# Scores of the next step beside the weights, value sums behind the masked scores, and the first batch of x in four pieces

## The chip, the cores and the metric

The kernel runs on one core of a Trainium2 chip. The metric is the device time of one execution in microseconds; less is better. Engines are named as in the profile: PE multiplies matrices (PEld is its weight load), DVE, ACT and POOL do elementwise work, SP issues DMA transfers.

## The reference

One decoder layer on x of 4 batches, 512 tokens, 512 features, in fp32. The part that the change touches is the first sublayer, a gated attention with 16 heads and 64 memory slots:

```python
def step_k(hk, x):
    q_t, k_t, p_t, g_t = x
    hk = hk * g_t[:, :, None, :] + k_t[..., None] * p_t[:, :, None, :]
    return (hk, jnp.einsum('bhk,bhkm->bhm', q_t, hk))
...
pvT = jax.nn.softmax(okT, axis=-1)
def step_v(hv, x):
    pv_t, v_t, p_t, g_t = x
    hv = hv * g_t[..., None] + p_t[..., None] * v_t[:, :, None, :]
    return (hv, jnp.einsum('bhm,bhmv->bhv', pv_t, hv))
...
o = o * jax.lax.rsqrt(jnp.mean(jnp.square(o), axis=-1, keepdims=True) + EPS) * g_norm_weight
o = o * (g * jax.nn.sigmoid(g))
return o.reshape(b, t, VALUE_DIM) @ Wo
```

q, k, s, v and g are projections of x. A cross attention over a context of 512 tokens and an MLP with quantised weights and activations and two Hadamard transforms follow, each with a residual and a layer norm.

## The kernel before

The program is written by hand, engine by engine, with semaphores; each engine walks the same list of stages (`attention_order`, then `seam_order`, then `ffn_order`) and emits its own part of each.

**Steps.** The first sublayer is 32 steps. A step is a pair of heads of one batch. The recurrences are done as sums over four blocks of 128 tokens, with a triangular mask inside a block. Step n's own stages are: `keys` (transposes of k and of exp(s)), `scores` (k times q for each head, 128x128 per block, masked by DVE into AM), `states` (running sums of k times p in HK, L485, and of p times v in HV, L490), `ok` (HK times q, L497, and exp(s) times the masked scores, L502, into one bank), `turn_ok`, a softmax, `turn_w`, `weights` (exp(s) times the softmax weights, L526, masked by DVE into the same AM, and HV times the weights, L534), `values` (AM times V, L540). Between them stand projections of step n+1 (`q`, `k`, `s`, `vg0` to `vg3`: 12 matmuls of 128x512 each, L431 to L433, three passes of a split fp32 product) and the output of step n-1 (`turn_o`, `y`: 24 such matmuls). The tuple `STEP` is this order; `OF_NEXT` names the stages that belong to step n+1.

**Shapes on PE.** Three kinds of matmul use the array differently. Most use all of it. `scores` and `weights` contract over 64 rows, one head in each half of the rows, side by side in time (64*128 in the profile: the row tiling). L490 and L502 write 64 columns for each head (128*64: the column tiling). In the profile two instructions stand for each matmul of an fp32 product with 128 columns.

**Banks.** PE's `take` hands out eight PSUM banks by due times from a table, `HOLD`; a bank is reused once the reader of its last content has counted its semaphore.

**Masks.** DVE's part of `scores` multiplies both heads' scores by the mask (L1008), its part of `weights` does it for the weights (L1048). In `values` it sums squares, POOL takes the root (L1337), then DVE gates the output (L1061).

**Beside the steps.** From step 24 on, `PLACES` puts the stages of the cross attention of each batch at numbered places (16 a step) of the stage list. `SEAM` is the order of the last step. `UNIT` is the order in the MLP. `tern` stages prepare the MLP's weights in the RAW buffers.

**Start.** SP first loads constants (C) and three vectors, then the list `first`: Wq, batch 0 of x in two halves (into AM and OG, free at that time), Wk, Ws, Wv and Wg, batch 1 of x, Wo. ACT rounds each piece to its high part, DVE subtracts to make the low part. A projection starts when all of x's batch and its weights have both parts.

Of the kernel before, what the change touches and what calls it, by code (L numbers as in the profile page):

```python
# [10 lines left out]
ALU = mybir.AluOpType  # L11
# [3 lines left out]
NB, T, D = 4, 512, 512  # L15
# [21 lines left out]
class Queue:  # L37
# [5 lines left out]
    def wait_ge(self, sem, value):  # L43
# [5 lines left out]
STEP = ("keys", "q", "scores", "states", "load_x", "tern", "k", "ok", "s", "turn_ok", "turn_o", "vg0", "tern",  # L49
        "turn_w", "vg1", "y", "weights", "vg2", "values", "tern", "vg3")  # L50
OF_NEXT = ("q", "k", "s", "vg0", "vg1", "vg2", "vg3")


def step_order(n, tasks):

    terns = 0
    for stage in STEP:
        m = n + 1 if stage in OF_NEXT else n - 1 if stage in ("turn_o", "y") else n
        if stage == "tern":
            terns += 1  # L60
            if n and terns in ((2,) if n + 1 in LAST else (1, 2, 3)):
                for t in tasks[:1]:
                    yield stage, t
                del tasks[:1]
        elif stage == "load_x":
            if n == 0:
                yield stage, 3
        elif 0 <= m < STEPS:
            yield stage, m
# [26 lines left out]

PLACED = [stage for stage in STEP if stage not in ("scores", "load_x", "tern")]


def attention_order():  # L100
# [3 lines left out]
    yield "load_x", 2  # L104
# [8 lines left out]
SEAM = (("keys", 31), ("scores", 31), ("states", 31), ("turn_o", 30), ("ok", 31), ("y", 30), ("turn_ok", 31), None,  # L113
# [7 lines left out]
def seam_order():  # L121

    for p, item in enumerate(SEAM):
        if item and item[0] == "unit":
            yield from ffn_place(item[1])
        elif item:
# [6 lines left out]
    dict(ctx=400, centre=403, n1=406, qk=408, qk_out=409, x101=414, x101_out=415, energy=418, x123=419,  # L133
         energy_out=419, att_scale=419, x123_out=420, att01=422, att01_out=423, att23=424, att23_out=426, xm0=430,
         xm0_out=431, xm1=433, xm1_out=434, xm2=435, xm2_out=436, xm3=438, xm3_out=439, x_round0=440, x_made0=443,
         x_round1=443, x_made1=445, x_turned=449, x_turned_out=450),
    dict(ctx=445, centre=445, qk=447, qk_out=448, n1=449, x101=450, energy=451, x101_out=452, energy_out=452,
         x123=454, att_scale=454, x123_out=455, att01=456, att01_out=457, att23=457, att23_out=458, xm0=459,
         xm0_out=461, xm1=463, xm1_out=464, xm2=464, xm2_out=465, xm3=465, xm3_out=466, x_round0=467, x_made0=468,
         x_round1=468, x_made1=471, x_turned=475, x_turned_out=476),  # L140
    dict(ctx=475, centre=476, n1=477, qk=479, qk_out=480, x101=481, x101_out=482, energy=483, energy_out=484,
         x123=486, att_scale=486, x123_out=487, att01=488, att01_out=489, att23=489, att23_out=490, xm0=492,
# [5 lines left out]
         x_round1=539, x_made1=541, x_turned=543, x_turned_out=544),  # L148
# [16 lines left out]
def beside(place):  # L165
# [5 lines left out]
UNIT = (("absmax", 25), ("had1_out", 5), ("clamp", 30), ("turn_q_out", 32), ("high", 2), ("low", 2), ("gate", 0),  # L171
        ("h", 1), ("had1", 4), ("had2_out", 24), ("read", 20), ("round", 29), ("gs", 0), ("scale", 28), ("add", 35),
        ("normal", 36), ("store", 38), ("turn_q", 31), ("had2", 23), ("down", 33), ("silu", 0))
# [4 lines left out]
HOLD = (("o", 11), ("en", 8), ("y", 8), ("vg", 8), ("xm", 7), ("gate", 6), ("up", 6), ("h1", 6), ("h2", 8), ("down",  # L178
        8), ("hq", 8), ("xt", 9), ("q", 5), ("k", 5), ("s", 5), ("sc", 8), ("wt", 8), ("ok", 12), ("okt", 7), ("w",
        8), ("ot", 8), ("kt", 7), ("et", 8), ("hk", 6), ("hv", 5), ("att", 10), ("x1", 9), ("qk", 8), ("spread", 8))  # L180
# [25 lines left out]
const_in vec_in raw0_in raw1_in am_in og_in v_in u_in y_in0 y_in1 y_in2 y_in3 ctx_in xw_in w3_in0 w3_in1 w3_in2 w3_store out_done  # L206
# [10 lines left out]
h_round hq_made hq_turned hq_evac0 hq_evac1 down ffn_add n3_stats n3_aggr n3_var n3_rstd n3_applied  # L217
# [3 lines left out]
def build(nc, x, xT, Wq, Wk, Wv, Wg, Ws, Wo, gw, cT, xWqT, xbq, xWkT, xbk, wgT, wuT, wdT, cst, out):  # L221
    with ExitStack() as top:
# [9 lines left out]
        def bank(*use):  # L232
# [106 lines left out]
        raw = {0: RAW[:, 0, :], 1: RAW[:, 1, :], "am": flat(AM[:]), "og": flat(OG[:]),  # L339
               "v": V[:, 1].rearrange("p i v -> p (i v)"), "u": U[:, 1].rearrange("p i v -> p (i v)")}  # L340
        raw_in = {0: S["raw0_in"], 1: S["raw1_in"], "am": S["am_in"], "og": S["og_in"], "v": S["v_in"], "u": S["u_in"]}
# [6 lines left out]
        first = [("Q", 0, 0), ("x", 0, 0, "am"), ("x", 0, 1, "og"), ("K", 0, 1), ("S", 0, 0), ("VG", 0, 0, "v"),  # L348
                 ("VG", 0, 1, "u"), ("x", 1, 0, "am"), ("x", 1, 1, "og"), ("WO", 0, 0),
# [4 lines left out]
        for key, where, _ in pieces:  # L354
            landings[where] = landings.get(where, 0) + (32 if key[0] == "VG" else 16)
            slot[key], landed[key] = where, landings[where]
# [5 lines left out]
        def left_raw(key):  # L362
            if key[0] == "x":
                return (S["x_lo_v"], 2 * key[1] + key[2] + 1) if key[1] < 2 else (S["x_lo_g"], 2 * key[1] + key[2] - 3)
# [29 lines left out]

        def x_parts(b, hc):
            cs = slice(2 * hc, 2 * hc + 2)
            return raw[slot["x", b, hc]].rearrange("p (c t) -> p c t", c=2), X[:, b, 0, cs, :], X[:, b, 1, cs, :]
# [11 lines left out]
        def tensor(engine):  # L409
# [18 lines left out]
            def passes(o, lh, ll, rh, rl, n):  # L428

                for c in range(n):  # L430
                    engine.matmul(o, lh(c), rh(c), start=c == 0, stop=False)  # L431
                    engine.matmul(o, lh(c), rl(c), start=False, stop=False)  # L432
                    last = engine.matmul(o, ll(c), rh(c), start=False, stop=c == n - 1)  # L433
                return last

            def project(kind, n, freed):
# [3 lines left out]
                pe.wait_ge(*left_raw(("x", b, 1)))  # L440
                weight_ready(pe, kind, n)
                passes(bk[:], lambda c: Wh[:, c, o:o + 128], lambda c: Wl[:, c, o:o + 128],
                       lambda c: X[:, b, 0, c, :], lambda c: X[:, b, 1, c, :], 4).then_inc(S["proj_" + kind.lower()], 1)

            def project_vg(n, i):
# [3 lines left out]
                weight_ready(pe, "VG", n)  # L449
                passes(bk[:], lambda c: X[:, b, 0, c, tl], lambda c: X[:, b, 1, c, tl],  # L450
                       lambda c: Wh[:, c, 384:896], lambda c: Wl[:, c, 384:896], 4).then_inc(S["proj_vg"], 1)

            def attend(stage, n):
# [15 lines left out]
                elif stage == "scores":  # L469

                    ba = [take(("sc", n, h), (S["a_masked"], 2 * n + h + 1)) for h in range(2)]
                    pe.wait_ge(S["q_evac"], n + 1)
                    for i in range(4):
# [5 lines left out]
                elif stage == "states":  # L479
                    bh = take(("hk", n), (S["hk_evac"], n + 1), (S["hk_add"], 2 * n + 2))  # L480
                    bv = take(("hv", n), (S["hv_evac"], n + 1), (S["hv_add"], 2 * n + 2))
# [4 lines left out]
                    mm.then_inc(S["hk_mm"], 1)  # L486
                    pe.wait_ge(S["v_evac"], 4 * n + 4)
# [222 lines left out]
        def scalar(engine):  # L710
# [39 lines left out]
            def attention(stage, n):  # L750
# [31 lines left out]
                elif stage == "states":  # L782
# [6 lines left out]
                    hk.then_inc(S["hk_evac"], 1)  # L789
                    act.wait_ge(S["hv_mm"], n + 1)  # L790
# [118 lines left out]
            for p in first[:10]:  # L909
# [5 lines left out]
            act.wait_ge(S["x_lo_v"], 4)  # L915
# [28 lines left out]
        def vector(engine):  # L944
            dve = Queue(engine)

            def x_low(b, hc):
                r, hi, lo = x_parts(b, hc)
                dve.wait_ge(S["x_hi"], 2 * b + hc + 1)
# [50 lines left out]

            def attend(stage, n):
                par = n % 2
                smv = sm[:, par]
                if stage == "scores":
                    for h in range(2):
                        dve.wait_ge(S["scores"], 2 * n + h + 1)
                        dve.wait_ge(S["ov_sum"], 2 * n)
                        engine.tensor_tensor(AM[:, h], bank("sc", n, h)[:].rearrange("p (i t) -> p i t", i=4), MB,  # L1008
                                             ALU.mult).then_inc(S["a_masked"], 1)
                elif stage == "states":  # L1010
                    bh, bv = bank("hk", n), bank("hv", n)
                    dve.wait_ge(S["hk_evac"], n + 1)
                    for i in (1, 2):
# [4 lines left out]
                        add.then_inc(S["hk_add"], 1)  # L1018
                    dve.wait_ge(S["hv_evac"], n + 1)
# [504 lines left out]
```

## Time and profile before

| | |
|---|---|
| median of 3 runs | 1557.42 us (1556.99 to 1559.42) |
| the profiled execution | 1557.25 us, its span 1555.1 us |
| PE busy | 1514.9 us, 97% |
| DVE busy | 1044.6 us, 67% |
| ACT busy | 653.5 us, 42% |
| POOL busy | 433.5 us, 28% |
| weights to weights, one step | 35.85 us |

The span is what the profiler covers; 2.15 us of the profiled execution's time lie outside it. An engine with a share near 100% has work nearly all the time, though not each kind of work is equally well packed. The clock line of the page is 9 in all 40 slices, that is 90% or more.

### The profile page before, as it was taken

What the parts mean: (1) busy time and instruction counts of PE and PEld (TensorE: products, weight loads), DVE (VectorE), ACT (ScalarE), POOL (GpSimd) and SP (SyncE); (2) the same over time, 40 slices, a digit from 0 to 9 for tenths busy, and PEclk for the clock granted to TensorE, in tenths of its full rate; (3) what the DMA queues carried; (4) which work ended last, traced back from release to release, by engine and by line L of the source; (5) the groups of instructions that cost most, each with busy time, mean ns of one, the idle gap of its engine ahead of it and who ended that gap; (6) DMA issues with size and microseconds to landing.
All of it is one profiled execution on the core that took longest, in us unless ns stands there. A gap on an engine that the chain in (4) does not pass through costs nothing.

```text
span 1555.1 us, 24171 instructions
## 1 busy us (share of the span) xinstructions
PE 1514.9 (97%) x9570; PEld 1208.2 (78%) x9570; DVE 1044.6 (67%) x1988; ACT 653.5 (42%) x1245; POOL 433.5 (28%) x282
## 2 busy tenths in 40 slices
PE   6999999999999999999999999998999889999997
PEld 5888888888888888888888888877888745666675
DVE  4555666555565566666566667777787976877887
ACT  4333333333323333333343333324243346867774
POOL 0211011110205444543444413122330234333320
PEclk9999999999999999999999999999999999999999
DMA  7212111111102122212223211101110403544552
GB/s 258 69 35 68 53 50 55 55 52 45 48 28 75 56 86 71 75 62 81 68 89 102 68 39 51 55 21 34 55 41 28 163 28 122 156 130 130 162 173 79
DMA packets 107551, 121.16 MB, mean 78 GB/s; under 512 B 5296, under 2 KB 75056, under 8 KB 107312
## 3 DMA queue, kind: packets, MB, share of 16 engines
q1 hardware_dynamic: 103984, 113.33, 22.7%
q10 hardware_dynamic: 3456, 6.29, 1.1%
q8 instruction: 76, 1.25, 0.3%
q14 instruction: 35, 0.29, 0.1%
HBM read 92.34 MB, written 27.26 MB: 77 GB/s over the span
## 4 chain that ended last, share of the span: by engine, by line
PE 89%; DVE 7%; issue 2%; ACT 1%; DMA 0%; POOL 0%; SPq 0%; POOLq 0%; DVEq 0%; ACTq 0%
PE bank L431 18%; PE bank L433 17%; PE bank L432 17%; PE bank L642 6%; PE bank L540 4%; PE bank L657 3%; PE bank L678 3%; PE bank L476 2%; PE bank L526 2%; PE bank L502 2%; PE bank L485 2%; PE bank L548 2%; PE bank L490 2%; PE bank L497 1%; PE bank L534 1%
## 5 line engine op out<-in xcount | busy, mean ns | idle before, releaser
L431 PE MATMUL bank<-Wh,X 128*128 128x512 f32 x512 | 211.5, 413 | 0.0
L433 PE MATMUL bank<-Wh,X 128*128 128x512 f32 x512 | 200.9, 392 | 0.0
L432 PE MATMUL bank<-Wl,X 128*128 128x512 f32 x512 | 200.3, 391 | 0.0
L769 ACT ACTIVATE V<-bank 128x256 f32<-128x256 f32 x128 | 49.2, 384 | 324.7 <-PE bank L433 324.5
L431 PE MATMUL bank<-X,Wh 128*128 128x512 f32 x384 | 161.6, 421 | 12.3 <-DVE X L950 12.3
L1337 POOL TENSOR_TENSOR sm<-sm,half 128x8 f32<-128x8 f32 x32 | 52.8, 1650 | 398.8 <-DVE sm L1055 398.8
L1319 POOL TENSOR_TENSOR Wl<-RAW,Wh 128x512 fp32r<-128x512 f32 (+1 forms) x65 | 112.7, 1742 | 140.7 <-ACT Wh L724 140.7
L433 PE MATMUL bank<-X,Wl 128*128 128x512 f32 x384 | 151.8, 395 | 0.0
L432 PE MATMUL bank<-X,Wh 128*128 128x512 f32 x384 | 150.5, 392 | 0.0
L642 PE MATMUL bank<-XT,W 128*128 128x512 bf16 x512 | 121.3, 381 | 3.0 <-DVE M L1208 3.0
L1360 POOL TENSOR_TENSOR LO<-M,HI 128x512 fp32r<-128x512 f32 x64 | 82.5, 1288 | 149.6 <-PE bank L651 119.3
L433 PEld LDWEIGHTS bank<-Wh,X 128*128 128x128 f32 x512 | 96.2, 188 | 21.3
L998 DVE SCALAR_TENSOR_TENSOR U<-U,bank 128x256 f32<-128x256 f32 x128 | 51.6, 403 | 90.3 <-ACT U L771 90.2
L431 PEld LDWEIGHTS bank<-Wh,X 128*128 128x128 f32 x512 | 96.5, 188 | 19.9
L432 PEld LDWEIGHTS bank<-Wl,X 128*128 128x128 f32 x512 | 96.7, 189 | 16.7
L1327 POOL TENSOR_SCALAR RAW<-RAW 128x1024 f32<-128x1024 f32 x24 | 87.1, 3628 | 75.9 <-ACT RAW L747 75.4
L996 DVE RECIPROCAL ZT<-ZT 128x512 f32<-128x512 f32 x32 | 107.3, 3353 | 1.1
L1061 DVE SCALAR_TENSOR_TENSOR OG<-bank,sm,U 128x128 f32<-128x128 f32 x256 | 69.2, 344 | 56.5 <-POOL sm L1337 56.5
L431 PE MATMUL bank<-Woh,OTh 128*128 128x512 f32 x256 | 99.9, 390 | 0.0
L431 PEld LDWEIGHTS bank<-X,Wh 128*128 128x128 f32 x384 | 72.7, 189 | 34.9 <-DVE X L950 12.3
L432 PE MATMUL bank<-Wol,OTh 128*128 128x512 f32 x256 | 99.6, 389 | 0.0
L433 PE MATMUL bank<-Woh,OTl 128*128 128x512 f32 x256 | 99.6, 389 | 0.0
(190 smaller groups left out, 3255.2 us busy)
## 6 DMA issues: line engine op xcount, KB each, us to landing
z_scratch<-EV SPq DMA_DIRECT2D x64, 256.0 KB, 2.0
Z<-z_scratch SPq DMA_DIRECT2D x16, 1024.0 KB, 5.8
RAW<-wgT SPq DMA_DIRECT2D x16, 512.0 KB, 3.7
RAW<-wuT SPq DMA_DIRECT2D x16, 512.0 KB, 3.7
RAW<-wdT SPq DMA_DIRECT2D x16, 512.0 KB, 3.6
RAW<-Wo SPq DMA_DIRECT2D x14, 512.0 KB, 3.5
RAW<-Wv SPq DMA_DIRECT2D x26, 256.0 KB, 2.9
RAW<-Wg SPq DMA_DIRECT2D x26, 256.0 KB, 3.2
```

Source lines behind the costliest of these rows:

```text
L431: engine.matmul(o, lh(c), rh(c), start=c == 0, stop=False)
L432: engine.matmul(o, lh(c), rl(c), start=False, stop=False)
L433: last = engine.matmul(o, ll(c), rh(c), start=False, stop=c == n - 1)
L540: mm = engine.matmul(bo[h][:, 128 * i:128 * i + 128], AM[:, h, i, :], V[:, par, i, 128 * h:128 * h + 128], start=False, stop=i == 3)
L642: mm = engine.matmul(bk[:], w[:, c, 128 * j:128 * j + 128], XT[b % 3][:, c, :], start=c == 0, stop=c == 3)
L996: engine.reciprocal(ZT[:], ZT[:]).then_inc(S["z_recip"], 1)
L998: engine.scalar_tensor_tensor(u, u, 1.0, bank("vg", n, i)[:, 256:512], ALU.add, ALU.mult).then_inc(S["u_made"], 1)
L1061: og = engine.scalar_tensor_tensor(OG[:, h, i, :], bank("o", n, h)[:, 128 * i:128 * i + 128], smv[:, 4, g:g + 1], U[:, par, i, 128 * h:128 ...
L1319: engine.tensor_tensor(lo, r, hi, ALU.subtract).then_inc(S["w_lo_g"], 1)
L1327: engine.tensor_scalar(r, r, MAGIC - 1.0, MAGIC + 1.0, ALU.max, ALU.min).then_inc(S["w3_clip"], 1)
L1337: engine.tensor_tensor(smv[:, 4, :], smv[:, 3, :], half[:, 0:8], ALU.pow).then_inc(S["o_rstd"], 1)
L1360: engine.tensor_tensor(LO[:, n % 2, :], M[n % 3], HI[:, n % 3, :], ALU.subtract).then_inc(S["h_lo"], 1)
```

## The change

`scores` becomes a stage of the next step and stands directly ahead of `weights`, behind `vg2`. The value sums leave `states` and become a stage of their own, `sums`, directly behind `ok`. DVE's masks of the scores of step n+1 are done inside `values` of step n, ahead of the wait for POOL's root. `vg2` is now ahead of `weights`, and nothing stands between `weights` and `values` on PE. Batch 0 of x comes in four pieces, ahead of the constants, and the projections of step 0 wait piece by piece. The tables HOLD and PLACES get other numbers, and UNIT another order, which leaves every engine's order in the MLP as it was. One semaphore takes the place of two in the last norm.

```diff
-STEP = ("keys", "q", "scores", "states", "load_x", "tern", "k", "ok", "s", "turn_ok", "turn_o", "vg0", "tern",
-        "turn_w", "vg1", "y", "weights", "vg2", "values", "tern", "vg3")
-OF_NEXT = ("q", "k", "s", "vg0", "vg1", "vg2", "vg3")
+STEP = ("keys", "q", "states", "k", "tern", "load_x", "ok", "sums", "s", "turn_ok", "turn_o", "vg0", "tern", "turn_w",
+        "vg1", "y", "vg2", "scores", "load_x", "weights", "values", "tern", "vg3")
+OF_NEXT = ("q", "k", "s", "vg0", "scores", "vg1", "vg2", "vg3")
...
-SEAM = (("keys", 31), ("scores", 31), ("states", 31), ("turn_o", 30), ("ok", 31), ("y", 30), ("turn_ok", 31), None,
+SEAM = (("keys", 31), ("states", 31), ("turn_o", 30), ("ok", 31), ("sums", 31), ("y", 30), ("turn_ok", 31), None,
...
-    dict(ctx=400, centre=403, n1=406, qk=408, qk_out=409, x101=414, x101_out=415, energy=418, x123=419,
+    dict(ctx=397, centre=403, n1=406, qk=408, qk_out=409, x101=414, x101_out=415, energy=417, x123=419,
...
-HOLD = (("o", 11), ("en", 8), ("y", 8), ("vg", 8), ("xm", 7), ("gate", 6), ("up", 6), ("h1", 6), ("h2", 8), ("down",
+HOLD = (("o", 10), ("en", 13), ("y", 8), ("vg", 9), ("xm", 9), ("gate", 7), ("up", 7), ("h1", 6), ("h2", 8), ("down",
...
-        first = [("Q", 0, 0), ("x", 0, 0, "am"), ("x", 0, 1, "og"), ("K", 0, 1), ("S", 0, 0), ("VG", 0, 0, "v"),
-                 ("VG", 0, 1, "u"), ("x", 1, 0, "am"), ("x", 1, 1, "og"), ("WO", 0, 0),
+        first = [("x", 0, 0, "am0"), ("Q", 0, 0), ("x", 0, 1, "am1"), ("x", 0, 2, "og0"), ("x", 0, 3, "og1"), ("K", 0, 1),
+                 ("S", 0, 0), ("VG", 0, 0, "v"), ("VG", 0, 1, "u"), ("x", 1, 0, "am"), ("x", 1, 1, "og"), ("WO", 0, 0),
...
+                made = None
+                if n == 0:
+
+                    made = lambda c: (((S["w_hi"], weight_no[kind, 0]), (S["x_hi"], c + 1)), left_raw(("x", 0, c)),
+                                      left_raw((kind, 0)))
...
                     pe.wait_ge(S["q_evac"], n + 1)
+                    pe.wait_ge(S["k_evac"], n + 1)
...
+            def mask(n):
+                for h in range(2):
+                    dve.wait_ge(S["scores"], 2 * n + h + 1)
+                    dve.wait_ge(S["ov_sum"], 2 * n)
+                    dve.wait_ge(S["const_in"], 16)
+                    engine.tensor_tensor(AM[:, h], bank("sc", n, h)[:].rearrange("p (i t) -> p i t", i=4), MB,
+                                         ALU.mult).then_inc(S["a_masked"], 1)
...
+                    if n + 1 < STEPS:
+                        mask(n + 1)
                     dve.wait_ge(S["o_rstd"], n + 1)
```

**PE, from scores to values.** In a step after the first, PE's order before has the scores (L476) between `q` and the two kinds of sums (L485 into HK, L490 into HV).

```order
L432 MATMUL bank<-X,Wh 128x512
L433 MATMUL bank<-X,Wl 128x512
L476 MATMUL bank<-QP,KT 128x128 x8
L485 MATMUL bank<-Et,Kt 128x128 x3
L490 MATMUL bank<-V,Et 64x128 x6
L431 MATMUL bank<-X,Wh 128x512
L432 MATMUL bank<-X,Wh 128x512
```

In the change the scores (L506) stand behind `vg2` and ahead of the weights (L557), HV times weights (L565) and values (L571).

```order
L448 MATMUL bank<-Wl,X 128x512
L451 MATMUL bank<-Wh,X 128x512
L506 MATMUL bank<-QP,KT 128x128 x8
L557 MATMUL bank<-WT,ET 128x128 x8
L565 MATMUL bank<-HV,WT 128x128 x6
L571 MATMUL bank<-V,AM 128x128 x8
L445 MATMUL bank<-Wh,X 128x512
```

Before, the rows of L526 and L534 stood behind `y`, and the 12 matmuls of `vg2` between L534 and the values at L540.

**DVE, from the output adds to the gating.** Before, behind the adds of `y` (L1079), with the semaphores that each row waits for:

```order
L1079 TENSOR_TENSOR Y<-Y,bank 128x512 [waits y_mm] x3
L1048 TENSOR_TENSOR AM<-bank,C 128x512 [waits weights] x2
L998 SCALAR_TENSOR_TENSOR U<-U,bank 128x256 [waits g_tanh]
L1052 TENSOR_REDUCE sm<-OG 128x2x4 [waits o_square]
L1055 SCALAR_TENSOR_TENSOR sm<-sm 128x8 [waits eps_total,o_square_sum]
L1061 SCALAR_TENSOR_TENSOR OG<-bank,sm,U 128x128 [waits o_rstd]
```

The same place in the change:

```order
L1030 SCALAR_TENSOR_TENSOR U<-U,bank 128x256 [waits g_tanh]
L1087 TENSOR_TENSOR AM<-bank,C 128x512 [waits weights] x2
L1091 TENSOR_REDUCE sm<-OG 128x2x4 [waits o_square]
L1094 SCALAR_TENSOR_TENSOR sm<-sm 128x8 [waits eps_total,o_square_sum]
L1038 TENSOR_TENSOR AM<-bank,C 128x512 [waits ov_sum,scores]
L1038 TENSOR_TENSOR AM<-bank,C 128x512 [waits scores]
L1103 SCALAR_TENSOR_TENSOR OG<-bank,sm,U 128x128 [waits o_rstd]
```

U of `vg2` is now ahead of the masks of the weights, and the masks of the next scores are between the mean square and the gating.

**SP, the first transfers.** Before:

```order
L1395 DMA C<-cst 128x5x128
L1396 DMA gwc<-gw 128x1
L1397 DMA XB<-xbq 128x1
L1398 DMA XB<-xbk 128x1
L1448 DMA RAW<-Wq 128x4x128
L1433 DMA AM<-xT 128x2x512
L1433 DMA OG<-xT 128x2x512
L1448 DMA RAW<-Wk 128x4x128
```

In the change the constants and the vectors stand behind Wv and Wg, ahead of batch 1 of x:

```order
L1475 DMA AM<-xT 128x512
L1490 DMA RAW<-Wq 128x4x128
L1475 DMA AM<-xT 128x512
L1475 DMA OG<-xT 128x512 x2
L1490 DMA RAW<-Wk 128x4x128
L1490 DMA RAW<-Ws 128x4x128
```

## Rows read from the trace of the kernel before

**Rows 1.** The page, part 4: shares of the chain that ended last.
```profile
PE 89%; DVE 7%; issue 2%; ACT 1%; DMA 0%; POOL 0%; SPq 0%; POOLq 0%; DVEq 0%; ACTq 0%
```

**Rows 2.** Windows: busy PE, PEld, DVE, ACT, POOL; then clock, DMA share, GB/s.
```profile
960.00:1260.00 300.00, 284.61 (x1775) 233.67 (x1773) 229.85 (x469) 115.60 (x234) 71.24 (x53) 0.98 0.16 54
```

**Rows 3.** Timeline of PE, one step: start us, us, instruction, [idle before].
```profile
305.99 1.16 PE L526 MATMUL bank<-WT,ET 64*128 64x128 f32 x16
306.99 0.84 PE L534 MATMUL bank<-HV,WT 64*128 64x128 f32 x12
307.75 0.50 PE L431 MATMUL bank<-Wh,X 128*128 128x512 f32 x1
...
310.61 1.95 PE L540 MATMUL bank<-V,AM 128*128 128x128 f32 x16
312.31 0.48 PE L431 MATMUL bank<-Wh,X 128*128 128x512 f32 x1
...
315.81 0.47 PE L431 MATMUL bank<-X,Wh 128*128 128x512 f32 x1
...
318.75 1.16 PE L476 MATMUL bank<-QP,KT 64*128 64x128 f32 x16
319.84 0.94 PE L485 MATMUL bank<-Et,Kt 128*128 128x128 f32 x6
320.71 0.88 PE L490 MATMUL bank<-V,Et 128*64 128x128 f32 x12
321.51 0.50 PE L431 MATMUL bank<-X,Wh 128*128 128x512 f32 x1
...
324.38 0.83 PE L497 MATMUL bank<-QP,HK 128*128 128x128 f32 x6
325.13 1.09 PE L502 MATMUL bank<-AM,Et 128*64 128x128 f32 x16
326.16 0.50 PE L431 MATMUL bank<-X,Wh 128*128 128x512 f32 x1
...
341.85 1.16 PE L526 MATMUL bank<-WT,ET 64*128 64x128 f32 x16
```

**Rows 4.** Timeline of DVE, same step.
```profile
304.70 2.47 DVE L1079 TENSOR_TENSOR Y<-Y,bank 128x512 f32<-128x512 f32 x4
...
311.50 0.42 DVE L998 SCALAR_TENSOR_TENSOR U<-U,bank 128x256 f32<-128x256 f32 x1 [3.02 <-ACT U L771]
...
316.39 2.16 DVE L1061 SCALAR_TENSOR_TENSOR OG<-bank,sm,U 128x128 f32<-128x128 f32 x8 [1.75 <-POOL sm L1337]
...
319.94 1.29 DVE L1008 TENSOR_TENSOR AM<-bank,C 128x512 f32<-128x512 f32 x2 [1.06 <-PE bank L476]
```

**Rows 5.** Timeline of all engines, 58.5 to 60 us.
```profile
58.78 1.28 DVE L1048 TENSOR_TENSOR AM<-bank,C 128x512 f32<-128x512 f32 x2
...
59.52 0.71 PE L540 MATMUL bank<-V,AM 128*128 128x128 f32 x4
```

**Rows 6.** Timeline of the first 35 us, all engines.
```profile
8.51 1.06 ACT L716 ACTIVATE X<-AM 128x1024 fp32r<-128x1024 f32 x1 [2.25 <-DMA AM<-xT]
...
12.33 0.79 PE L431 MATMUL bank<-X,Wh 128*128 128x512 f32 x1 [12.33 <-DVE X L950]
...
17.61 0.63 PE L431 MATMUL bank<-X,Wh 128*128 128x512 f32 x1
...
18.36 0.39 PE L433 MATMUL bank<-X,Wl 128*128 128x512 f32 x1
...
21.74 0.58 ACT L755 ACTIVATE QP<-bank 128x512 f32<-128x512 f32 x1
...
34.26 0.49 PE L463 MATMUL bank<-C,KT 128*128 128x128 f32 x3
```

**Rows 7.** Waits of PE from 960 to 1260 us.
```profile
PE bank L540 <- DVE AM L1048: 3.0, 2, 2.8
```

**Rows 8.** Timeline of all engines, 1048 to 1052 us.
```profile
1049.05 1.78 DVE L1169 TENSOR_SCALAR ax<-ax 128x2 f32<-128x2 f32 x1
```

More of the change, by code:

```diff
@@ L65, in step_order @@
         elif stage == "load_x":
+            loads += 1
             if n == 0:
-                yield stage, 3
+                yield stage, loads + 1
         elif 0 <= m < STEPS:
@@ L93, in raw_tasks @@
     yield STEPS - 1, ("WO", LOADS - 1)
-PLACED = [stage for stage in STEP if stage not in ("scores", "load_x", "tern")]
+PLACED = [stage for stage in STEP if stage not in ("scores", "sums", "load_x", "tern")]
 def attention_order():
@@ L354, in build @@
         for key, where, _ in pieces:
-            landings[where] = landings.get(where, 0) + (32 if key[0] == "VG" else 16)
-            slot[key], landed[key] = where, landings[where]
+            n = raw_in[where].name
+            landings[n] = landings.get(n, 0) + (32 if key[0] == "VG" else 16)
+            slot[key], landed[key] = where, landings[n]
         weight_no = {key: i + 1 for i, key in enumerate(key for key, _, _ in pieces if key[0] not in "xF")}
@@ L486, in attend @@
                     mm.then_inc(S["hk_mm"], 1)
+                elif stage == "sums":
+                    bv = take(("hv", n), (S["hv_evac"], n + 1), (S["hv_add"], 2 * n + 2))
                     pe.wait_ge(S["v_evac"], 4 * n + 4)
@@ L789, in attention @@
                     hk.then_inc(S["hk_evac"], 1)
+                elif stage == "sums":
                     act.wait_ge(S["hv_mm"], n + 1)
@@ L907, in ffn @@
                                       ACT.Copy).then_inc(S["hq_evac0"], 1)
-            for p in first[:10]:
+            for p in first[:12]:
                 if p[0] == "x":
@@ L913, in scalar @@
                     w_high(p[:-1])
-            act.wait_ge(S["x_lo_v"], 4)
+            act.wait_ge(S["x_lo_v"], 6)
             act.wait_ge(S["w_lo_v"], 5)
@@ L1004, in attend @@
                 if stage == "scores":
[L1005 to L1009, printed above, removed]
+                    if n == 0:
+                        mask(0)
                 elif stage == "states":
-                    bh, bv = bank("hk", n), bank("hv", n)
+                    bh = bank("hk", n)
                     dve.wait_ge(S["hk_evac"], n + 1)
@@ L1018, in attend @@
                         add.then_inc(S["hk_add"], 1)
+                elif stage == "sums":
+                    bv = bank("hv", n)
                     dve.wait_ge(S["hv_evac"], n + 1)
@@ L1270, in attention @@
                     attend(stage, n)
-            dve.wait_ge(S["const_in"], 16)
             engine.memset(half[:, 0:16], -0.5).then_inc(S["vec_made"], 1)
             engine.memset(half[:, 16:17], MAGIC).then_inc(S["vec_made"], 1)
-            for p in first[:10]:
+            for p in first[:12]:
                 if p[0] == "x":
@@ L1425, in sync @@
                     placed.add(2)
-                if where in held:
-                    sp.wait_ge(*left_raw(held[where]))
-                held[where] = key
+                buffer = {"am0": "am", "am1": "am", "og0": "og", "og1": "og"}.get(where, where)
+                if buffer in held and where == buffer:
+                    sp.wait_ge(*left_raw(held[buffer]))
+                held[buffer] = key
                 r, done = raw[where], raw_in[where]
```

105 lines of the change are left out of this document (61 added, 44 removed).

## The prediction

> **What bounds the kernel now.** I read the page's chain first: PE holds 89% of it [rows 1]. Then the windows: in most of the attention PE is busy all the time, and from 960 to 1260 us, where the cross attention stands beside the steps, 284.6 of 300 us, with DVE at 229.9 [rows 2]. So up to step 23 a step costs what PE's instructions cost, and I priced it from PE's timeline. From weights to weights a step takes 341.85 - 305.99 = 35.86 us [rows 3]. There is no wait in it, but it has places where the array changes its use: all rows, two halves of the rows, two halves of the columns.
>
> **The price of a change of tiling.** An instruction of 128 columns costs 0.106 us in a full group (values: 16 in 1.70 [rows 3]), and a side-by-side pair costs about 0.11. L526, 8 pairs, takes 1.00: 0.12 for entering. L534, 6 pairs, stays in the same tiling and takes 0.76: 0.10 for leaving. L476 enters and leaves: 1.09 for 8 pairs, 0.21 over. L485, six full instructions after it and before the columns, takes 0.87 for 0.66; L490, 6 pairs, 0.80; L497 0.75 for 0.66; L502, 8 pairs, 1.03 [rows 3]. The run of 12 projections ahead of the row tiling takes 2.94, the one after the columns 2.87, 2.86 after the rows, about 0.09 and 0.02 more than plain. Both sides of a boundary together cost about 0.18 us, and a step before has eight such boundaries: into and out of rows twice, into and out of columns twice. The change leaves four.
>
> The Trainium skill (TensorEngine Tiling (Array Packing), Key Properties) says that a change of the tiling mode, not of the tile alone, drains the engine. By the trace it agrees: L526 to L534 changes operands but not the tiling, and costs nothing. TensorE: Matmul & The Clock Gate (Single matmul latency), also of the Trainium skill, puts the constant part of one matmul at 166 ns; taken as the drain, an estimate, four boundaries would give 0.66 us a step, against 0.76 in the sum below.
>
> **The step, term by term** (all from [rows 3]). L476 no longer leaves its tiling: 1.09 to 1.00. L526 no longer enters it: 1.00 to 0.90. Values follow L534 directly and now pay the entry that L485 paid: 1.70 to 1.80. L485 stands between projections: 0.87 to 0.59 (six at 0.11, less the 0.08 by which a full group overlaps its successor). L502 does not leave the columns, L490 does not enter: 1.03 to 0.92, 0.80 to 0.75. Projection runs: 0.09, 0.02 and 0.02 less, and 0.12 for vg2, which joins the run of y. Sum: -0.09 -0.10 +0.10 -0.28 -0.11 -0.05 -0.25 = -0.78, of which I keep -0.76, the differences being rounded to 0.01.
>
> **The wait that the change adds.** Before, 2.86 us of vg2 covered DVE's masks between weights and values; now only L534's 0.76 does. DVE starts a mask 0.03 us after PE's group is shown to end (319.94 against 318.75 + 1.16 [rows 3, 4]), so 0.19 after L534's start (305.99 + 1.16 + 0.03 - 306.99). Values started 0.74 after the mask did in the one early step where PE waited for it [rows 5]. That makes 0.93 against 0.76: 0.17 us of wait, once; the second head's mask is 0.6 later, and the first head's eight instructions take 0.9. Net per step: -0.76 + 0.17 = **-0.59**. Behind the waiting instruction are vg3 and all of PE; they shift by the 0.17 too.
>
> Is DVE free by then? U of vg2 now stands ahead of the masks. It ends 1.31 us after vg2's successor starts (311.50 + 0.42 - 310.61), the masks are wanted 1.00 + 0.90 + 0.19 = 2.09 after it, so 0.8 us are left. The adds of y ended at 307.17, 1.18 after PE left y [rows 4]; 2.8 us of vg2 now stand between, and DVE sat idle 3.02 us there. The masks of the next scores, 1.29 us, go into DVE's wait of 1.75 for POOL [rows 4]: nothing on the path. If POOL slowed them, the gating would be late by so much, and it is first needed by the next `ok`, which takes over its bank. The sums into HK had 3.67 us from L485's end to `ok` (324.38 - 320.71) and now have one projection run, 2.85: 0.82 less. But DVE's adds stood behind the scores' masks, which ended at 321.23 [rows 4] and are now out of the way, so they can start up to 1.29 earlier. HV's adds have until the weights. Bounds of the net: -0.76 if the wait is hidden in leaving the tiling, -0.3 if the wait is half a microsecond.
>
> The GPSIMD Engine Reference of the Trainium skill (Specifications) says that POOL shares its SBUF interfaces with VectorE's 2-port modes and with instructions of two SBUF inputs. By that rule a mask, with one input in PSUM, runs freely beside POOL, as priced; [rows 8] show the other sort, a 128x2 tensor_scalar that took 1.78 us.
>
> **The sum over steps.** Steps 0 to 23: 24 x 0.59 = 14.2 us. Steps 24 to 30 could give 7 x 0.59 = 4.1, and the last step 1.6 (the scores of step 31 have moved out, 1.09 + 0.2 of boundaries, and 0.3 for the sums). But there DVE is often the one that is waited for [rows 2], and what PE saves is partly waited away. One stall speaks the other way: DVE's weights masks were 2.8 us late near 1049 [rows 7], after a small DVE instruction beside POOL [rows 8]; with vg2 and scores ahead of the weights DVE has caught up there, but the next x1 transposes wait for the same DVE chain. I take 4.6 of 5.7 and bounds of 0 and 10.
>
> **The start.** Before, PE starts at 12.33, as x comes after 320 KB of constants and is split in halves of 512 KB (the first landed at 8.51) [rows 6]. By 8.51, 1.09 MB had landed. In the change, x's first quarter and Wq, 0.5 MB, lead: both should be there at about 5, and PE starts at 5.5 to 6. All of x (1.25 MB with Wq) is there at about 9, and PE follows piece by piece. At the start its matmuls run at the 1.2 GHz level (one is shown with 0.63 us at 17.61, 0.43 apart), and from 18.36 on at the 2.4 GHz level (shown with 0.39, 0.23 apart) [rows 6], so it works for 6 us at the lower one. It has 48 matmuls (q, k, s, vg0) before the scores, and should be through at 19 to 21. But scores of step 0 now need q and k copied by ACT, and these copies stand behind all of `first` on ACT, batch 1 of x and Wo among it: before, q's copy started at 21.74 [rows 6]. The constants, 320 KB, still precede batch 1, and the transfers ran without a gap, so these copies move by about 1 us only: q's at 20.7, k's done at 21.8. Then the scores, 1.3 us with boundaries, and 36 matmuls, 8.3 us: `keys` at 31.4 against 34.26 [rows 6], **-2.9 us** with the scores already in. Bounds: 0, when the copies do not move and the wait puts the clock at its lower level, and -5, when they move by 3. The output adds and the F pieces get their data later by the new transfer order, but their first use is a step away.
>
> **MLP and tail.** The order of every engine there is the same by the listing; other banks by HOLD: 0, bounds ±1.
>
> **Total.** -2.9 - 14.2 - 4.6 = -21.7 against the profiled execution's own 1557.25 (span 1555.1 and 2.15 around it), which is the runs' median, 1557.42, within 0.2: **1535.5 us**.
>
> **Rivals.**
> - *A: the early start is lost.* PE reaches the scores early, waits for q's copy, and the clock falls to its lower level. For: the copies stand behind Wo. Against: the wait is 1 to 3 us. Start gives 0.5: 1538.
> - *B: DVE gives it back.* Between 960 and 1260 DVE paces, and nothing of the 4.6 comes: 1540. For: DVE's 230 of 300 us; against: PE's 285.
> - *C: stalls there vanish too.* The 2.8 us stall [rows 7] goes with others like it, and the region gives 9: 1531.
> - *D: the change does not do what it says.* Scores and weights side by side still drain at each head's or stage's change, and only sums save (0.2 a step): 1535.5 + 31 x 0.39 = 1547.5. Against: L526 to L534.
> - *E, the other side: slower.* DVE comes late to the weights masks in every step, as U of vg2 and y's adds stand ahead and vg2 no longer covers. It decides from 0.7 us a step (31 x 0.7 = 21.7) beyond the 0.17, that is with DVE 1.5 us later than I see it; at 1.5 beyond, +46.5: 1582. Against: the 3.02 idle [rows 4].
>
> **How the numbers follow.** Forecast 0.50 (its own range 1533 to 1538), A 0.14, B 0.14, C 0.15, D 0.04, E 0.03. The likeliest gives 1535.5. The range runs from beyond C (1530, with the start's upper bound partly taken) to B and a little more, as the bounds of the wait allow +/-4: 1528 to 1543. It leaves D, E and the far ends out, under 2 in 10. Faster or slower means by over 0.2%, 3.1 us, about what a measurement of this kernel can tell: A to D are all faster; E and surprises are slower. Faster 0.95, same 0.02, slower 0.03.
>
> **What would show it.** Weights to weights in 35.27 us in steps 2 to 23; L565 to L571 0.93 apart with a short wait for DVE; L506 to L557 and L533 to L521 without a boundary; `keys` of step 0 at 31.4 with a wait of 1 to 3 us ahead of the first scores; DVE's wait for POOL shrunk from 1.75 to about 0.5. It is wrong if PE waits elsewhere in a plain step (for a bank, or for HK), or if waits from 960 to 1260 grow beyond 15 us.

## The result and the profile after

The changed kernel took 1549.52 us (median of 6 runs, 1545.90 to 1553.01), against 1557.22 us for the kernel before (6 runs, 1556.53 to 1559.42) on the same chip: ratio 0.9947, 95% interval 0.9932 to 0.9963. That is faster, as forecast, but by 7.7 us and not by 22: 14.0 us above the 1535.5 of the prediction and outside its range. The profiled execution took 1548.67 us, with a span of 1546.9.

The chain that ended last (page, part 4) has less PE in it than before [rows 1], and 2% each of DMA and ACT instead of 0% and 1%, work that PE had to wait for:

```profile
PE 86%; DVE 7%; issue 2%; ACT 2%; DMA 2%; POOL 1%; SPq 0%; POOLq 0%; DVEq 0%; ACTq 0%
```

I measured the steps first, from the start of one weights stage to the next, over the whole attention. All values are worked out from PE's timeline; the last column is what the prediction says for the stretch.

| stretch | before | after | difference | forecast |
|---|---|---|---|---|
| span's start to the first weights (step 0) | 54.66 | 58.66 | +4.0, of which 2.86 is vg2 moved in | -2.9 |
| first to 25th weights (24 steps) | 860.99 | 859.57 | -1.4 | -14.2 |
| 25th to 32nd weights (beside the cross attention) | 324.90 | 315.29 | -9.6, of which 2.86 is vg2 moved out | -4.6, with the next |
| last weights to the end | 314.55 | 313.38 | -1.2 | (in -4.6) |

So the start and the first 24 steps failed, and the crossed steps gave more than forecast (-6.7 and -1.2 against -4.6). A plain step, however, is the one that was forecast. PE's timeline of one, the same step as [rows 3] (start us, us, instruction):

```profile
305.53 1.16 PE L506 MATMUL bank<-QP,KT 64*128 64x128 f32 x16
306.52 1.06 PE L557 MATMUL bank<-WT,ET 64*128 64x128 f32 x16
307.42 0.84 PE L565 MATMUL bank<-HV,WT 64*128 64x128 f32 x12
308.36 2.05 PE L571 MATMUL bank<-V,AM 128*128 128x128 f32 x16
...
316.53 0.83 PE L514 MATMUL bank<-Et,Kt 128*128 128x128 f32 x6
...
319.97 0.83 PE L528 MATMUL bank<-QP,HK 128*128 128x128 f32 x6
320.73 1.09 PE L533 MATMUL bank<-AM,Et 128*64 128x128 f32 x16
321.65 0.82 PE L521 MATMUL bank<-V,Et 128*64 128x128 f32 x12
```

L506 to L557 is 0.99 (forecast 1.00), L557 to L565 0.90 (0.90), L565 to L571 0.94 (0.93, with the wait), L533 to L521 0.92 (0.92). From weights to weights a plain step takes 35.31 to 35.33 us (forecast 35.27, before 35.85). But the list of the 24 steps is not plain throughout: a step in which the next pair's weights are made takes 35.6 (one of them 35.8), where such steps of the kernel before took 35.85 like all others (that one 36.0), and from the 19th step on the list reads 39.16, 37.53, 35.61, 36.95, 37.58, 35.61. These six take 222.4 us, 10.5 more than six plain ones. The waits of PE over the whole kernel name the place:

```profile
PE bank L528 <- DVE HK L1053: 6.6, 4, 1.7
PE bank L445 <- ACT Wh L755: 5.8, 1, 5.8
PE bank L506 <- ACT KT L791: 4.9, 1, 4.9
```

Four waits at `ok` (L528) for DVE's adds into HK, 6.6 us, and one of 4.9 us of the first scores for ACT's copy of k (the 5.8 is the wait for the first data). The first of the four, timeline of all engines:

```profile
703.03 2.01 ACT L755 ACTIVATE Wh<-RAW 128x1024 fp32r<-128x1024 f32 x2
704.17 4.76 POOL L1360 TENSOR_TENSOR Wl<-RAW,Wh 128x1024 fp32r<-128x1024 f32 x2 [0.66 <-ACT Wh L755]
706.02 0.60 ACT L786 ACTIVATE QP<-bank 128x512 f32<-128x512 f32 x1
709.34 0.63 ACT L755 ACTIVATE Wh<-RAW 128x512 fp32r<-128x512 f32 x1 [2.73 <-DMA RAW<-Wq]
709.88 0.43 ACT L819 ACTIVATE HK<-bank 64x64 f32<-64x64 f32 x2
710.35 0.95 DVE L1053 TENSOR_TENSOR HK<-bank,HK 64x64 f32<-64x64 f32 x4 [4.31 <-ACT HK L819]
711.44 0.91 PE L528 MATMUL bank<-QP,HK 128*128 128x128 f32 x6 [1.73 <-DVE HK L1053]
712.28 1.42 PE L533 MATMUL bank<-AM,Et 128*64 128x128 f32 x16
```

Read it from below. PE waits for DVE, but DVE had been idle for 4.31 us, waiting for ACT's copy into HK. That copy took its turn behind the high part of the next pair's Wq, and this waited 2.73 us for the transfer of Wq. (SP issued that transfer only at 706.60. Its waits there name POOL's low parts, L1360, whose first one had just ended: the buffer was not free before.) The wait's name says DVE; its cause is ACT's queue. The other three are alike: ACT waits 2.73, 2.08 and 2.75 us for Wq, and PE 1.73, 1.38 and 1.75 us.

The kernel before has ACT's wait too, four times (2.60, 2.47, 2.11 and 2.63 us), and PE doesn't wait there at all. Its second one, timeline of ACT, DVE and PE:

```profile
749.25 0.60 ACT L755 ACTIVATE QP<-bank 128x512 f32<-128x512 f32 x1
752.32 0.63 ACT L724 ACTIVATE Wh<-RAW 128x512 fp32r<-128x512 f32 x1 [2.47 <-DMA RAW<-Wq]
752.86 0.43 ACT L788 ACTIVATE HK<-bank 64x64 f32<-64x64 f32 x2
753.33 0.95 DVE L1016 TENSOR_TENSOR HK<-bank,HK 64x64 f32<-64x64 f32 x4 [1.70 <-ACT HK L788]
754.77 0.83 PE L497 MATMUL bank<-QP,HK 128*128 128x128 f32 x6
```

DVE's adds ended at 754.28, 0.49 us before PE came to `ok`. From q's copy to `ok` PE had 5.52 us of other work there; in the step above it has 3.69 (711.44 - 1.73 - 706.02), as the scores and the value sums have moved out.

In the first of the four waits the clock fell as well. L533 then takes 1.42 us instead of 1.09: the granted clock is at the 1.2 GHz level from 712.9 to 716.3.

The start, timeline of PE, ACT and SP:

```profile
23.73 2.08 PE L506 MATMUL bank<-QP,KT 64*128 64x128 f32 x16 [4.92 <-ACT KT L791]
...
29.32 0.63 PE L451 MATMUL bank<-Wh,X 128*128 128x512 f32 x1
...
36.12 0.49 PE L492 MATMUL bank<-C,KT 128*128 128x128 f32 x3
```

```profile
16.77 1.06 ACT L747 ACTIVATE X<-AM 128x1024 fp32r<-128x1024 f32 x1 [2.02 <-DMA AM<-xT]
18.08 1.06 ACT L747 ACTIVATE X<-OG 128x1024 fp32r<-128x1024 f32 x1 [0.26 <-DMA OG<-xT]
21.16 1.06 ACT L755 ACTIVATE Woh<-RAW 128x1024 fp32r<-128x1024 f32 x1 [2.02 <-DVE RAW L988]
22.12 0.29 ACT L950 ACTIVATE IDB<-C 128x128 bf16<-128x128 f32 x1
22.32 0.29 ACT L951 ACTIVATE H<-C 128x128 fp32r<-128x128 f32 x1
22.52 0.58 ACT L786 ACTIVATE QP<-bank 128x512 f32<-128x512 f32 x1
23.00 0.59 ACT L791 ACTIVATE KT<-bank 128x512 f32<-128x512 f32 x1
```

```profile
9.02 0.47 SPq L1445 DMA_DIRECT2D C<-cst  x1
...
10.58 0.43 SPq L1448 DMA_DIRECT2D XB<-xbk  x1
11.06 0.43 SPq L1475 DMA_DIRECT2D AM<-xT  x1
```

PE was through with the 48 projections at 18.8, a little ahead of the forecast (19 to 21); the last of them started 7.4 us earlier than before (18.43 against 25.87). Then it waited 4.92 us: q's copy ran at 22.52, not at 20.7, and the scores ran at the lower clock level (2.08 us instead of 1.16), as did the ten projections behind them (0.43 apart until 30.2). `keys` of step 0 came at 36.12, 4.7 after the forecast 31.4, and 1.9 after the 34.26 of before [rows 6].

### The profile page after: what moved, and what is told of

It reads as the page before. It is cut to its first block, busy times and chain, and to the rows that moved or that the text cites. A ratio compares the mean times of both kernels' runs of the same rounds, so it can differ in the third digit from the quotient of the medians.

```text
span 1546.9 us, 24193 instructions
## 1 busy us (share of the span) xinstructions
PE 1498.8 (97%) x9570; PEld 1207.3 (78%) x9570; DVE 1043.6 (67%) x1990; ACT 651.8 (42%) x1247; POOL 434.2 (28%) x282
## 4 chain that ended last, share of the span: by engine, by line
PE 86%; DVE 7%; issue 2%; ACT 2%; DMA 2%; POOL 1%; SPq 0%; POOLq 0%; DVEq 0%; ACTq 0%
PE bank L445 17%; PE bank L451 17%; PE bank L448 17%; PE bank L673 6%; PE bank L571 4%; PE bank L688 3%; PE bank L709 3%; PE bank L506 2%; PE bank L533 2%; PE bank L557 2%; PE bank L579 2%; DVE AM L1087 1%; PE bank L528 1%; PE bank L521 1%; PE bank L514 1%
## 5 line engine op out<-in xcount | busy, mean ns | idle before, releaser
L1360 POOL TENSOR_TENSOR Wl<-RAW,Wh 128x512 fp32r<-128x512 f32 (+1 forms) x65 | 112.7, 1743 | 134.0 <-ACT Wh L755 134.0
L673 PEld LDWEIGHTS bank<-XT,W 128*128 128x128 bf16 x512 | 49.0, 99 | 57.3 <-issue 5.9
```

Source lines behind the costliest of these rows:

```text
L673: mm = engine.matmul(bk[:], w[:, c, 128 * j:128 * j + 128], XT[b % 3][:, c, :], start=c == 0, stop=c == 3)
L1360: engine.tensor_tensor(lo, r, hi, ALU.subtract).then_inc(S["w_lo_g"], 1)
```

## The experiments

Each was timed in 5 rounds against the kernel before. "Median" is that of its own runs, 4 to 6 of them. Experiments 1 to 4 ran on one chip, 6 to 9 on a second, 5, 10 and 11 on a third; the kernel before had medians of 1557.12, 1557.62 and 1556.90 us there, so medians of different chips are comparable to about 0.7 us only, and the ratios, each against the kernel before on the same chip, are the better measure. The lengths of steps are those of the one profiled execution of each kernel.

**Experiment 1: ACT's queue at `ok`.** The next Wq is made one stage later, behind k's copy:

```diff
-    return {"q": [("Q", l + 1)], "k": [("K", l + 1)], "s": [("S", l + 1)], "y": [("WO", l + 1)],
+    return {"k": [("Q", l + 1), ("K", l + 1)], "s": [("S", l + 1)], "y": [("WO", l + 1)],
```

> The changed kernel, with the high and low parts of the next pair's Wq one stage later (behind the copy of k, ahead of Wk's, instead of ahead of the copy into HK). Theory: in steps 18 to 24 ACT waits for Wq's transfer (2.0 to 2.75 us) with the copy into HK queued behind it, DVE adds late and PE waits at ok: four waits of 1.76 to 2.14 us, and a stretch at the lower clock. With the copy ahead of that wait these go: the steps from 18 to 24 give back 8 to 10 us, 1549.5 becomes 1539.5 to 1541.5. Rival 1, DVE itself is the late one (its adds queued behind its other work): the waits at ok stay and the time stays at 1549.5. Rival 2, the wait moves: ACT now waits with the copy of ok behind it, PE waits at the turns instead, and under 3 us come back.

Median 1542.81 us (1540.09 to 1544.86), ratio 0.9908 (0.9893 to 0.9923). The same place in its timeline:

```profile
706.73 0.45 ACT L819 ACTIVATE HK<-bank 64x64 f32<-64x64 f32 x2 [0.38 <-PE bank L514]
707.21 0.95 DVE L1053 TENSOR_TENSOR HK<-bank,HK 64x64 f32<-64x64 f32 x4 [1.44 <-ACT HK L819]
709.28 0.83 PE L528 MATMUL bank<-QP,HK 128*128 128x128 f32 x6
709.48 0.60 ACT L791 ACTIVATE KT<-bank 128x512 f32<-128x512 f32 x1 [2.31 <-PE bank L451]
709.98 0.62 ACT L755 ACTIVATE Wh<-RAW 128x512 fp32r<-128x512 f32 x1
```

The copy into HK comes as soon as PE has made the states, DVE adds at once, L528 waits for nothing, and Wq has landed by the time ACT comes to it. No wait at L528 for DVE is left in the kernel. The 24 steps take 850.5 us against 859.6: 9.0 back, which is the theory's size. The crossed steps took 3.6 us more in this execution (318.9 against 315.3), and what follows them 1.8 more, so its span is 4.0 shorter; by the medians the kernel gave 6.7, not 8 to 10. That the rest has to do with this edit is not shown. Rival 1 (DVE itself late) is out, and rival 2 (the wait moves to the turns) too.

**Experiment 2: the copies of step 0.** ACT copies q and k of step 0 ahead of batch 1's x and Wo:

```diff
-            for p in first[:12]:
+            for at_, p in enumerate(first[:12]):
+                if at_ == 9:
+                    attention("q", 0)
+                    attention("k", 0)
...
+                elif n == 0 and stage in ("q", "k"):
+                    pass
```

> The changed kernel, with ACT's copies of q and k of step 0 ahead of the high parts of batch 1's x and of Wo, and nothing else. Theory: the first scores waited 4.92 us for these copies, queued on ACT behind batch 1 (k's copy at 23.0), and the clock fell to its lower level for 6.8 us after it, worth 3.4 us. Copies at about 16 to 18 us take both away: keys of step 0 from 36.08 to about 29, 1549.5 to 1542.5. Rival: transfers, not the queue, set the start, so that PE waits for batch 1 of x one stage later instead: keys of step 0 stays within 2 us of 36.

Median 1541.98 us (1540.23 to 1544.03), ratio 0.9907 (0.9893 to 0.9922): 7.5 us less, as expected. The timelines of ACT and PE:

```profile
14.93 0.58 ACT L786 ACTIVATE QP<-bank 128x512 f32<-128x512 f32 x1
15.41 0.59 ACT L791 ACTIVATE KT<-bank 128x512 f32<-128x512 f32 x1
...
19.66 1.16 PE L506 MATMUL bank<-QP,KT 64*128 64x128 f32 x16
...
29.05 0.49 PE L492 MATMUL bank<-C,KT 128*128 128x128 f32 x3
```

The scores start 4.07 us earlier, and `keys` 7.07 us earlier. The other 3.0 us lie between the two, where the same instructions take 9.39 us instead of 12.39: that is what the lower clock cost after the wait. Batch 1's x was not late for anything.

**Experiment 3: both.**

> Both edits: next Wq one stage later, copies of q and k of step 0 first. If the two waits are the whole of the 14 us between forecast and result, they add up: 1549.5 - 9 - 7 = 1533.5, range 1531 to 1537. If anything else of that size was missed (a price of the tiling change under 0.18 us in the steps, waits from 960 us on), it stays at 1540 or more.

Median 1536.21 us (1533.78 to 1538.19), ratio 0.9866 (0.9853 to 0.9879). 13.3 of the 14.0 us between forecast and result come back with two moves on ACT's queue; the two alone gave 6.7 and 7.5. That the total comes so near the forecast is in part luck: `keys` of step 0 now stands at 29.2, 2.2 ahead of the forecast, and the crossed steps and the rest are 2.3 under it, which makes up for 24 steps that are still 3.7 over it (850.5, forecast 846.8).

**Experiment 4: the new order with the old start.** The kernel before with the new order of stages, seam, places, units and holds.

> The kernel before with the new order of stages, seam, places, units and bank holds, but the old start (constants first, x in halves). Theory: the start of the changed kernel is worth about nothing or a small loss (keys of step 0 1.8 us later than before), so this part alone gives all of the gain: 1547 to 1550, with scores of step 0 in already. If the new start were worth what was forecast (2.9 us), it would be at 1552 or above.

Median 1548.47 us (1546.90 to 1552.78), ratio 0.9949 (0.9936 to 0.9962). All of the measured gain is in the order; the new start brought nothing to it. The first weights stand at 56.86 here and at 58.66 in the changed kernel, so beside the new order the new start lost 1.8 us.

**Experiment 5: the new start with the old order.** In the old order the scores of step 0 come after 36 more projections.

> The kernel before with the new start only (x of batch 0 in four pieces ahead of the constants, first projections piece by piece), order of stages as before, so that the scores of step 0 come after keys and not ahead of vg1. Theory: the new start is good by itself and was lost to the scores that now stand ahead of vg1: here PE has 36 more matmuls (8.3 us) to do while ACT gets to the copies, waits for nothing, and keys of step 0 stands at 27 to 28 instead of 34.26: 1557.4 - 6.5 = 1551, range 1549 to 1553. Rival (a start with earlier x is worth nothing here, as batch 1 and Wo come no earlier): 1557.

Median 1550.22 us (1548.31 to 1551.95), ratio 0.9962 (0.9950 to 0.9974): 6.7 us less than before. ACT's copy of q is as late as in the changed kernel, but `keys` needs no more than it has:

```profile
22.74 0.58 ACT L783 ACTIVATE QP<-bank 128x512 f32<-128x512 f32 x1
...
27.41 0.49 PE L491 MATMUL bank<-C,KT 128*128 128x128 f32 x3
```

27.41 against 34.26 [rows 6]. The new start is worth 6.9 us alone, and the new order undid it: the scores ahead of vg1 are what made a late copy into a wait.

**Experiment 6: scores apart from weights.** On the kernel of experiment 3, the row tiling is left after scores and entered again before weights:

```diff
-        "vg1", "y", "vg2", "scores", "load_x", "weights", "values", "tern", "vg3")
+        "vg1", "y", "scores", "vg2", "load_x", "weights", "values", "tern", "vg3")
```

> The kernel with both edits (1536.2 us), but scores stand ahead of vg2 and weights behind it, so that the row tiling is left and entered once more in each step. By the price of 0.18 us for both sides of a boundary this gives 2 x 0.18 = 0.37 us a step, 31 steps: 11.5 us more, 1547.7. Rival (side-by-side pairs drain at each stage's change anyway, and the gain of the change lay in the sums alone): no change, 1536.2.

Median 1550.49 us (1547.50 to 1550.80), ratio 0.9950 (0.9936 to 0.9964): 14.3 more. A plain step takes 35.75 instead of 35.32, 0.43 for two boundaries. PE's timeline shows its parts:

```profile
119.07 1.16 PE L506 MATMUL bank<-QP,KT 64*128 64x128 f32 x16
120.16 0.50 PE L445 MATMUL bank<-Wh,X 128*128 128x512 f32 x1
...
123.11 1.16 PE L557 MATMUL bank<-WT,ET 64*128 64x128 f32 x16
124.10 0.84 PE L565 MATMUL bank<-HV,WT 64*128 64x128 f32 x12
```

Scores now take 1.09 instead of 0.99 (leaving), weights 0.99 instead of 0.90 (entering), and the 12 projections in between 2.95, where 12 more in one run cost 2.72: 0.23. The price is real, 0.21 for each boundary, and somewhat above the 0.18 that I had read from before. The rival is out.

**Experiment 7: sums behind states again.** The other pairing undone, on the kernel of experiment 3:

```diff
-STEP = ("keys", "q", "states", "k", "tern", "load_x", "ok", "sums", "s", "turn_ok", "turn_o", "vg0", "tern", "turn_w",
+STEP = ("keys", "q", "states", "sums", "k", "tern", "load_x", "ok", "s", "turn_ok", "turn_o", "vg0", "tern", "turn_w",
```

> The kernel with both edits (1536.2 us), but sums follow the states directly again, between projections, instead of the masked scores' product in the same column tiling. One column tiling more to enter and leave in each step: 0.2 to 0.3 us a step by the prediction's terms, 31 steps, 6 to 9 us more: 1542 to 1545. Rival (columns cost nothing to enter, only rows do): 1536.

Median 1545.94 us (1544.92 to 1547.09), ratio 0.9924 (0.9912 to 0.9936): 9.7 more. A plain step takes 35.66, 0.34 more, again for two boundaries (into the columns and out of them), 0.17 each. Column tilings cost nearly what row tilings do. Of the 9.7 us the first 24 steps have 7.9 (858.5 against 850.5).

**Experiment 8: DVE's mask covered.** vg2 stands between weights and values, as before the change; scores and weights stay together.

```diff
-        "vg1", "y", "vg2", "scores", "load_x", "weights", "values", "tern", "vg3")
+        "vg1", "y", "scores", "load_x", "weights", "vg2", "values", "tern", "vg3")
```

> The kernel with both edits (1536.2 us), but vg2 stands behind the weights again, ahead of values, as in the kernel before, while scores and weights stay side by side: boundaries as many as before this edit, and the wait of values for DVE's first mask covered. If the 0.17 us at the end of the second weights line is that wait, each step is 0.17 shorter: 5.3 us less, 1531. If it is the price of leaving the row tiling and not a wait, the time stays at 1536.

Median 1544.63 us (1543.52 to 1547.20), ratio 0.9918 (0.9904 to 0.9931): 8.4 more, where 5.3 less was expected. The expected part is there: a plain step takes 35.15 instead of 35.32, so 0.17 us was the wait for the mask and not a price of the tiling. But the crossed steps take 334.2 us against 316.2, of which 2.86 is vg2 moved in: 15.2 more. PE's waits from 960 to 1260 us now begin with

```profile
PE bank L557 <- DVE Y L1126: 4.9, 4, 2.7
PE bank L445 <- POOL X1h L1393: 4.2, 1, 4.2
PE bank L445 <- DVE OG L1108: 3.8, 4, 1.7
```

The waits for DVE's adds of y (0.6 us in experiment 3) and for OG (none there) have grown by 8.1 us: without vg2 ahead of them, scores and weights reach DVE's results too early. That is about half of the 15.2. The other half stays open; the tables `PLACES` and `HOLD` were left as they are for the other order, and whether others would do better is not tested. So in the crossed steps the changed order helps at least in part because it puts 2.86 us of projections ahead of the point where PE meets DVE.

**Experiment 9: Wv and Wg behind the copies.** On the kernel of experiment 3, the loading steps:

```diff
-            "vg3": [("VG", l + 1, 0), ("VG", l + 1, 1)]}.get(stage, [])
+            "keys": [("VG", l + 1, 0), ("VG", l + 1, 1)]}.get(stage, [])
```

> The kernel with both edits (1536.2 us), and the high and low parts of the next pair's Wv and Wg behind the copies of Kt and Et instead of ahead of them. Theory: steps that load weights are 0.3 us longer than the others, as ACT's two high parts (2.0 us) stand ahead of these copies and the states wait. Some 13 steps load, so 2 to 4 us less: 1532 to 1534. Rival: the parts are then late for vg0 (POOL's low parts take 2.7 us each), PE waits there, and it is slower than 1536.

Median 1534.18 us (1532.93 to 1535.49), ratio 0.9848 (0.9835 to 0.9862). The loading steps among the first 24 now take 35.33 (one of them 35.49), and these 24 steps 848.1 instead of 850.5. The crossed steps took 2.5 us more in the profiled execution, and the interval overlaps that of experiment 3: the step is mended, that the kernel gained is not shown.

**Experiments 10 and 11: the cover in the plain steps only.** On the kernel of experiment 9; the second one also makes Wv and Wg at vg3 again from step 22 on.

```diff
+COVERED = STEP[:16] + ("scores", "load_x", "weights", "vg2", "values", "tern", "vg3")
...
-    for stage in STEP:
+    for stage in COVERED if n < 22 else STEP:
```

> The kernel with Wv and Wg behind the copies (1534.2 us), and vg2 behind the weights in the steps up to 21 only; from 22 on, where cross attention stands beside the steps, the order of the changed kernel. Theory: covering DVE's mask is worth 0.17 us a step, and the 15 us that it cost in every step came from the crossed steps alone, where DVE paces: 22 x 0.17 = 3.7 us less, 1530.5. Rival: vg2 moved out leaves DVE late for good, and the first crossed steps are longer by some us: 1534 or more.

> As the last one, but from step 22 on the next Wv and Wg are made at vg3 again, since with these parts at keys the crossed steps took 2.4 us longer in one place (50.75 us against 48.36). Theory: 0.3 us comes back in the two or three loading steps from 22, and 2.4 goes: 2 us under the last one, 1528.5. Rival: the 2.4 us were scatter between two executions: no difference.

Medians 1532.39 us (1530.38 to 1535.32; ratio 0.9853, 0.9834 to 0.9871) and 1530.04 us (1527.51 to 1531.61; ratio 0.9830, 0.9815 to 0.9845). Plain steps take 35.15 in both, the crossed steps 318.1 and 317.3, and the profiled executions have the same span, 1528.6 and 1528.7, against 1531.9 of experiment 9. The cover gives 3.3 us there, near the expected 3.7. The ratio of experiment 10, however, is no lower than that of experiment 9 (0.9853 against 0.9848), so that this kernel gained by the cover is seen in one execution and not shown by the medians. Between the two nothing is told apart in the traces, where 2 us were expected: the step of 50.75 us became 49.91, and the two loading steps from 22 on took 0.6 more. The last one has the lowest median of the study, 27 us under the kernel before and some 19 under the changed one.

## Why the prediction was wrong, step by step

- **Price of a change of tiling (0.18 for both sides, four saved): right.** Before, a plain step takes 35.85, with the mask's wait covered 35.15: 0.70 for the four, forecast 0.76. Added back, the two row boundaries cost 0.43 (experiment 6) and the two column boundaries 0.34 (experiment 7): 0.77 together, so a boundary costs 0.17 to 0.21 us by its kind and place. The estimate of 0.66 that the 166 ns of the Trainium skill gave (TensorE: Matmul & The Clock Gate, Single matmul latency) lies as near to 0.70 as my sum; no run here shows that those 166 ns are what is paid.
- **The wait for the first mask, 0.17: right**, 0.17 by experiment 8. My bound that it might hide in leaving the tiling is excluded. DVE's wait for POOL came out as forecast too (0.55 us, forecast about 0.5).
- **Steps 0 to 23, -14.2: the step that failed most.** It reads "The sums into HK had 3.67 us from L485's end to `ok` ... and now have one projection run, 2.85: 0.82 less. But DVE's adds stood behind the scores' masks ... so they can start up to 1.29 earlier." I weighed DVE's queue and left out ACT's. The adds follow ACT's copy into HK, and this one follows, in the last step of each pair, the making of the next Wq, which waits for a transfer. One step in four has that at first; from the 19th step on nearly every one, and there the transfer is late. I had priced one plain step and multiplied by 24. The kernel before had the same late Wq on ACT; the scores and the value sums stood between q and `ok` there and covered it, with 0.49 us to spare in the step shown above. That was cover that the change took away, and I had costed it at nothing: 9.0 us (experiment 1), and 2.4 for Wv and Wg ahead of the copies of Kt and Et (experiment 9). The rest of the 12.8 is for the most part 24 times the 0.05 by which a plain step is longer than forecast.
- **The start, -2.9: wrong in its last link.** First matmul at 5.8 and projections done at 18.8 were right. The failed sentence is "the transfers ran without a gap, so these copies move by about 1 us only: q's at 20.7". They moved the other way, to 22.52. SP's rows show why the transfer of batch 1 was not issued earlier: its slot was free at 7.14, when DVE's second low part ended, but SP issued Wv, Wg and the four constants first and came to it at 11.06, against 10.85 before. It also took longer to land, by 16.77 against 15.88. And the transfers did not run without a gap: the DMA share is 0.68 from 6 to 8 us and 0.77 from 9 to 10, where the kernel before has 0.85 and 1.17. This is read from rows; no run tests which of these made the copies late. The wait I had put at 1 to 3 us was 4.9, and the clock fell, 3.0 us more. Rival A, which had 0.14, describes it, and its price of 2.4 us was too low: `keys` came 4.7 later than forecast.
- **Steps 24 to 31, -4.6: mis-sized.** It was -7.9. DVE did not give it back (rival B): PE's waits from 960 to 1260 us add up to 15.2 us before and after, so the 5.7 that I had cut to 4.6 came in full. The other 2.2 stay open. The number is nearer to rival C, but C's mechanism did not happen: the stall of 2.8 us is still there, with 2.1. Experiment 8 shows that vg2 ahead of the weights is part of why DVE keeps up.
- **MLP, 0:** with the tail -1.2, of which the last step's share was in my -4.6.
- Rivals D and E are out: experiments 6 and 7 show both pairings paying, and DVE was never late at the masks of a plain step beyond 0.17.

The sum of what was missed: 4.0 at the start, 12.8 in the 24 steps, 3.3 the other way in the rest, which makes 13.5 of the 14.0; the other 0.5 is between the profiled execution and the medians. What stays open is what sets the length of the crossed steps: in experiments 1 to 3, whose edits lie elsewhere, it was 318.9, 315.3 and 316.2 us, and I can't say for a given edit which way it goes.

## What to carry to other kernels

A saving read from one step holds for the steps that look like it: list the length of every step of the kernel before, and look at those in which something else (new weights, a load) stands in a queue. When work is taken out from between a producer and its consumer, follow the producer back through every in-order queue, waits for transfers in them included, and not only through the engine that the wait will be named after. And an earlier start is worth what the first consumer that can't start early leaves of it; here it was 6.9 us or less than nothing, by the place of one stage.

## What the runs showed of the hardware

- A wait of 4.92 us of PE was followed by 6.8 us at the 1.2 GHz level (granted clock 0.50; from 23.4, when it still stood idle, to 30.2), which cost 3.0 us on top. Before the wait PE's projections had stood 0.23 us apart since 9.8, and 0.43 apart ahead of that, as they do at the 1.2 GHz level behind the wait; the granted clock in the profile reads 1.00 in both stretches, so for the start the level is read from the distances alone. Of the four waits at `ok` (1.73, 1.73, 1.38 and 1.75 us), the first was followed by 3.4 us at the lower level, and the clock's records show no such stretch at the other three.
- Of two instructions of the same shape, one in a run of its tiling and one beside a boundary, the timeline shows the same duration (1.16 us for 16 of L506, in experiments 3 and 6). The boundary shows only in the distance of the starts, 0.99 against 1.09.
